# Block 0's VectorE and GpSimd work in another order, a reordered head, and the logits bias as a TensorE product

## What is computed

```python
h = gelu(embedding @ W0 + b0); h = gelu(h @ W1 + b1)
att = softmax(h @ W2 + b2)                       # 64 sequences x 8 kernels
agg_w = einsum('bk,koi->boi', att, weight[..., 0]); agg_b = att @ bias_k
hid = einsum('boi,bih->boh', agg_w, x) + agg_b[:, :, None]     # x: (64, 32, 512)

s = relu(hid @ up_w) ** 2                        # 512 -> 1024
shared = s @ down_w                              # 1024 -> 512
lat = hid @ fc1_w                                # 512 -> 256
routed = (lat @ expert_w) * sum(top2(hid @ gate_w)) @ fc2_w
out = x + layernorm(shared + routed) * ln_gamma + ln_beta
```

## Time and profile before

| what | value |
|---|---|
| median of 3 runs | 257.34 us (257.14 to 257.56) |
| the profiled execution: its time, its span | 257.82 us, 256.0 us |
| TensorE matmul busy | 248.1 us (97%), 1293 instructions |
| VectorE, ScalarE, GpSimd busy | 159.0 us (62%), 81.4 us (32%), 47.5 us (19%) |
| chain that ended last, by engine | TensorE 83%, VectorE 9%, issue 3%, DMA 2%, ScalarE 1% |

### The profile page before, as it was taken

The page is one execution under the profiler, slowest core; times in us unless marked ns, Lnnn a source line. Parts: engine busy times, 40 slices in busy tenths (PEclk is TensorE's granted clock), DMA queues, the critical chain, the costliest instruction groups (busy, mean ns, idle before and its releaser), DMA issues.

```text
span 256.0 us, 3526 instructions
## 1 busy us (share of the span) xinstructions
PE 248.1 (97%) x1293; PEld 207.0 (81%) x1293; DVE 159.0 (62%) x270; ACT 81.4 (32%) x141; POOL 47.5 (19%) x48
## 2 busy tenths in 40 slices
PE   7899999999999999999999999999999999999992
PEld 6778877988888888888888888888888888788891
DVE  4699999964448974544446984474444963406453
ACT  5567747530113344321111443331111355202100
POOL 2404083001115320001113501001111700001110
PEclk9999999999999999999999999999999999999998
DMA  6992805001111400001100220000111100000211
GB/s 146 352 358 93 320 0 165 3 0 44 41 41 41 141 25 0 3 0 42 41 38 16 80 112 0 0 0 0 41 41 44 42 0 0 3 0 2 80 44 41
DMA packets 10428, 15.60 MB, mean 61 GB/s; under 512 B 1072, under 2 KB 4912, under 8 KB 10416
## 3 DMA queue, kind: packets, MB, share of 16 engines
q1 hardware_dynamic: 9968, 15.33, 17.7%
q10 hardware_dynamic: 448, 0.11, 0.2%
HBM read 11.23 MB, written 4.20 MB: 60 GB/s over the span
## 4 chain that ended last, share of the span: by engine, by line
PE 83%; DVE 9%; issue 3%; DMA 2%; ACT 1%; POOL 0%; SPq 0%; POOLq 0%; DVEq 0%; ACTq 0%
PE ps L913 25%; PE ps L915 25%; PE ps L914 25%; PE ps L888 4%; DVE sq_lo L694 3%; DMA experts_sb<-in_experts_dram 2%; PE ps L980 2%; PE ps L841 2%; DVE y_buf L656 1%; DVE up_lo L626 1%; DVE down_lo L771 1%; PE ps L894 1%; DVE agg L663 0%; ACT up_hi L471 0%; DVE sq_hi L692 0%
## 5 line engine op out<-in xcount | busy, mean ns | idle before, releaser
L913 PE MATMUL ps<-down_hi,sq_hi 128*128 128x512 f32 (+1 forms) x136 | 51.2, 377 | 0.0
L914 PE MATMUL ps<-down_lo,sq_hi 128*128 128x512 f32 (+1 forms) x136 | 51.2, 377 | 0.0
L915 PE MATMUL ps<-down_hi,sq_lo 128*128 128x512 f32 (+1 forms) x136 | 51.2, 376 | 0.0
L913 PE MATMUL ps<-h_hi,up_hi 128*128 128x512 f32 x126 | 49.1, 390 | 0.2 <-DVE h_lo L647 0.2
L914 PE MATMUL ps<-h_lo,up_hi 128*128 128x512 f32 x126 | 49.0, 389 | 0.0
L915 PE MATMUL ps<-h_hi,up_lo 128*128 128x512 f32 x126 | 49.0, 389 | 0.0
L423 POOL TENSOR_TENSOR rstd<-mv,half 128x1 f32<-128x1 f32 x16 | 15.3, 954 | 158.1 <-DVE mv L726 153.1
L522 ACT ACTIVATE relu_sq<-ps 128x512 f32<-128x512 f32 x32 | 19.1, 597 | 58.2 <-PE ps L915 44.3
L719 DVE TENSOR_TENSOR y_buf<-ps,y_buf 128x512 f32<-128x512 f32 x15 | 10.4, 692 | 39.5 <-PE ps L915 39.3
L692 DVE CAST sq_hi<-relu_sq 128x512 fp32r<-128x512 f32 x32 | 22.6, 705 | 15.8 <-ACT relu_sq L524 15.2
L694 DVE TENSOR_TENSOR sq_lo<-relu_sq,sq_hi 128x512 fp32r<-128x512 f32 x32 | 30.9, 965 | 1.1
(11 more groups left out here) (136 smaller groups left out, 300.4 us busy)
## 6 DMA issues: line engine op xcount, KB each, us to landing
out_dram<-late SPq DMA_DIRECT2D x15, 256.0 KB, 2.0
x_cur<-in_x_dram SPq DMA_DIRECT2D x3, 1024.0 KB, 5.2
late<-in_down_w_dram SPq DMA_DIRECT2D x4, 512.0 KB, 5.0
late<-in_up_w_dram SPq DMA_DIRECT2D x3, 512.0 KB, 8.2
x_cur<-in_x_dram SPq DMA_DIRECT2D x2, 512.0 KB, 6.3
agg_b<-aggb_dram SPq DMA_DIRECT2D x1, 768.0 KB, 5.9
latents_sb<-in_latents_dram SPq DMA_DIRECT2D x1, 528.0 KB, 5.3
experts_sb<-in_experts_dram SPq DMA_DIRECT2D x1, 512.0 KB, 5.2
```

The source lines that it names most:

```text
L913: nc.tensor.matmul(dst, a_hi, b_hi, start=first, stop=False)
L914: nc.tensor.matmul(dst, a_hi, b_lo, start=False, stop=False)
L915: return nc.tensor.matmul(dst, a_lo, b_hi, start=False, stop=last)
```

## The change

It consists of these parts.

- The load of `b2_rows` and VectorE's addition go. `bias_sb`, the load of bias_k, has behind each row of bias_k eight more columns, of which row 0 holds b2 and the others are zero. A product of ones (`idle`) with these eight rows starts the accumulation of `LOGIT`, and the product with w2 ends it. The maximum and the exponential read `LOGIT` itself.
- Three idle products are added behind `WEIGHT_T`, and the third `fold_expert` call moves behind the transpose.
- `FIRST_BIAS` moves ahead of the last chunk of the first mix's first half. Behind it, on ScalarE and VectorE, the second piece of the up weights moves behind the copy of the bias and behind the first h.
- The up products of m = 0 and 1 of block 0 do the two products with `h_hi` before the one with `h_lo`, in all four chunks (before: in the first alone), and wait for `up_lo` piece by piece.
- In block 0, VectorE does `fc1_lo` and the first `x_plus_beta` itself, and squares, aggregate and down weights come in another order; on ScalarE the `down_high` calls come behind m = 3, 4 and 5, and `q_high` behind m = 6 and 7. Blocks 1 to 3 are as before.

```diff
-            sp.dma_start(b2_rows[:, :], kernels[0, C * C + C:C * C + C + K].partition_broadcast(NB)
-                         ).then_inc(b2_loaded, 16)
...
@@ GpSimd @@
-            pool.wait_ge(fc1_hi_ready, 1)
-            nc.gpsimd.tensor_tensor(fc1_lo[:, :, :], fc1_raw, fc1_hi[:, :, :].bitcast(fp32),
-                                    ALU.subtract).then_inc(fc1_lo_ready, 1)
...
-            def pool_block(b):
+            next_mix(0)
+            pool.wait_ge(mix_ready, G)
+            inverse_deviations(0)
+            with pool.Fori(1, NBLK - 1) as b:
                 x_plus_beta(b)
                 next_mix(b)
...
@@ ScalarE @@
-            act.wait_ge(logit_ready, 1)
             act.wait_ge(max_done, 1)
-            nc.scalar.activation(att_exp[:, :], logit_sb[:, :], ACT.Exp, bias=neg_max[:, :],
+            nc.scalar.activation(att_exp[:, :], LOGIT, ACT.Exp, bias=neg_max[:, :],
                                  accum_out=exp_sum[:, :]).then_inc(exp_done, 1)
...
             split_up(0)
-            split_up(1)
             act.wait_ge(bias_spread, 1)
             nc.scalar.copy(agg_b[:, 0:TOK], FIRST_BIAS).then_inc(bias_copied, 1)
+            split_up(1)
...
             for m in range(IC):
                 relu_square(0, m)
-                if m < 4:
-                    down_high(m)
+                if m == 3:
+                    down_high(0)
+                    down_high(1)
                 if m in (4, 5):
-                    q_high(m - 4)
+                    down_high(m - 2)
+                if m in (6, 7):
+                    q_high(m - 6)
...
@@ VectorE @@
-            dve.wait_ge(b2_loaded, 16)
-            nc.vector.tensor_tensor(logit_sb[:, :], LOGIT, b2_rows[:, :], ALU.add).then_inc(logit_ready, 1)
-            dve.wait_ge(logit_ready, 1)
-            nc.vector.tensor_reduce(neg_max[:, :], logit_sb[:, :], AX.X, ALU.max, negate=True).then_inc(max_done, 1)
+            nc.vector.tensor_reduce(neg_max[:, :], LOGIT, AX.X, ALU.max, negate=True).then_inc(max_done, 1)
...
             split_up(0)
-            split_up(1)
             dve.wait_ge(bias_copied, 1)
             first_mix_bias(0)
+            split_up(1)
             first_mix_bias(1)
...
+            def first_x_plus_beta():
+
+                dve.wait_ge(affine_loaded, 16)
+                dve.wait_ge(first_x_loaded, 16)
+                dve.wait_ge(x_loaded, 16)
+                dve.wait_ge(down_hi_ready, 2)
+                dve.wait_ge(down_lo_ready, 2)
+                nc.vector.tensor_tensor(x_beta, x_cur[:, :, :], beta_b.unsqueeze(1).to_broadcast([P, TB, HID]),
+                                        ALU.add).then_inc(xbeta_ready, 1)
...
@@ TensorE @@
+            pe.wait_ge(bias_loaded, 16)
+            nc.tensor.matmul(LOGIT, idle[0:K, 0:NB].bitcast(fp32), b2_row, start=True, stop=False)
             pe.wait_ge(gelu_done, 2)
-            nc.tensor.matmul(LOGIT, hid2[:, :], w2_sb, start=True, stop=True).then_inc(logit_done, 1)
+            nc.tensor.matmul(LOGIT, hid2[:, :], w2_sb, start=False, stop=True).then_inc(logit_done, 1)
...
+            stay_warm(3)
             pe.wait_ge(experts_loaded[0], 16)
             fold_expert(0, 0, 0)
             fold_expert(0, 0, 1)
-            fold_expert(1, 0, 0)
...
-            for c in range(HC):
+            for c in range(HC - 1):
                 first_mix_tiles(c, (0, 1))
             pe.wait_ge(attb_lo_ready, 2)
             pe.wait_ge(attP_copied, 1)
             nc.tensor.matmul(FIRST_BIAS, ones[:, :], bias_rows, start=True, stop=True).then_inc(bias_spread, 1)
+            first_mix_tiles(HC - 1, (0, 1))
...
-                pe.wait_ge(up_lo_ready, 2)
-                pe.wait_ge(h_hi_ready, 1)
...
+                for c in range(HC):
+                    pe.wait_ge(h_hi_ready, c + 1)
+                    for m in (0, 1):
+                        cols = slice(m * P, (m + 1) * P)
+                        pe.wait_ge(up_lo_ready, m + 1)
+                        nc.tensor.matmul(ps[:, UP_BANK[m], :], up_hi[:, c, cols], h_hi[:, c, :],
+                                         start=(c == 0), stop=False)
+                        nc.tensor.matmul(ps[:, UP_BANK[m], :], up_lo[:, c, cols], h_hi[:, c, :],
+                                         start=False, stop=False)
                     pe.wait_ge(h_lo_ready, c + 1)
                     for m in (0, 1):
-                        last = up_chunk(m, c)
+                        last = nc.tensor.matmul(ps[:, UP_BANK[m], :], up_hi[:, c, m * P:(m + 1) * P], h_lo[:, c, :],
+                                                start=False, stop=(c == HC - 1))
```

More of the change, by code:

```diff
@@ L148, in adaln_ffn_kernel @@
         bias_raw = bias_sb[:, 0:C]
+        b2_row = bias_sb[0:K, C:C + K]
         idle = sb("idle", [P, P], f32r)
-        b2_rows = sb("b2_rows", [NB, K])
-        logit_sb = sb("logit_sb", [NB, K])
         sel_g = sb("sel_g", [NB, G])
@@ L212, in adaln_ffn_kernel @@
         experts_loaded = [sem(f"experts_loaded{i}") for i in range(2)]
-        b2_loaded = sem("b2_loaded")
         x_loaded = sem("x_loaded")
@@ L240, in adaln_ffn_kernel @@
         padded = sem("padded")
-        logit_ready = sem("logit_ready")
         weightT_done = sem("weightT_done")
@@ L414, in x_plus_beta @@
                 pool.wait_ge(x_loaded, 16 * (b + 1))
-                wait_past(pool, final_done, TB * b)
+                pool.wait_ge(final_done, TB * b)
                 nc.gpsimd.tensor_tensor(x_beta, x_cur[:, :, :],
@@ L425, in _ @@
             pool.wait_ge(affine_loaded, 16)
-            pool.wait_ge(first_x_loaded, 16)
-            pool.wait_ge(down_hi_ready, 2)
-            pool.wait_ge(down_lo_ready, 2)
-            def pool_block(b):
+            next_mix(0)
+            pool.wait_ge(mix_ready, G)
+            inverse_deviations(0)
+            with pool.Fori(1, NBLK - 1) as b:
                 x_plus_beta(b)
@@ L433, in pool_block @@
                 inverse_deviations(b)
-            pool_block(0)
-            with pool.Fori(1, NBLK - 1) as b:
-                pool_block(b)
             x_plus_beta(NBLK - 1)
@@ L772, in down_low, with fc1_low @@
                                         ALU.subtract).then_inc(down_lo_ready, 1)
+            def fc1_low():
+                dve.wait_ge(fc1_hi_ready, 1)
+                nc.vector.tensor_tensor(fc1_lo[:, :, :], fc1_raw, fc1_hi[:, :, :].bitcast(fp32),
+                                        ALU.subtract).then_inc(fc1_lo_ready, 1)
+            def first_x_plus_beta():
[6 more added lines that the diff above has]
+                                        ALU.add).then_inc(xbeta_ready, 1)
+            split_square(0, 0)
             spread_aggregate(0)
+            split_square(0, 1)
             sum_aggregate(0)
-            for m in range(IC):
-                split_square(0, m)
-                if m < 4:
-                    down_low(m)
-                if m in (4, 5):
-                    q_low(m - 4)
+            split_square(0, 2)
+            fc1_low()
+            split_square(0, 3)
+            down_low(0)
+            down_low(1)
+            first_x_plus_beta()
+            split_square(0, 4)
+            down_low(2)
+            split_square(0, 5)
+            down_low(3)
+            split_square(0, 6)
+            q_low(0)
+            split_square(0, 7)
+            q_low(1)
             latent_low(0)
@@ L875, in _ @@
                                 ident[0:NB, 0:NB]).then_inc(attT_done, 1)
+            fold_expert(1, 0, 0)
             fold_expert(1, 0, 1)
@@ L881, in _ @@
             fold_expert(1, 1, 1).then_inc(q_done, 1)
-            pe.wait_ge(bias_loaded, 16)
             pe.wait_ge(attT_copied, 1)
@@ L925, in up_first_block @@
                 pe.wait_ge(bias_copied, 1)
-                pe.wait_ge(up_lo_ready, 2)
-                pe.wait_ge(h_hi_ready, 1)
-                for m in (0, 1):
-                    cols = slice(m * P, (m + 1) * P)
-                    nc.tensor.matmul(ps[:, UP_BANK[m], :], up_hi[:, 0, cols], h_hi[:, 0, :], start=True, stop=False)
-                    nc.tensor.matmul(ps[:, UP_BANK[m], :], up_lo[:, 0, cols], h_hi[:, 0, :], start=False, stop=False)
-                pe.wait_ge(h_lo_ready, 1)
-                for m in (0, 1):
-                    nc.tensor.matmul(ps[:, UP_BANK[m], :], up_hi[:, 0, m * P:(m + 1) * P], h_lo[:, 0, :],
-                                     start=False, stop=False)
-                for c in range(1, HC):
+                for c in range(HC):
[7 more added lines that the diff above has]
+                                         start=False, stop=False)
                     pe.wait_ge(h_lo_ready, c + 1)
                     for m in (0, 1):
-                        last = up_chunk(m, c)
+                        last = nc.tensor.matmul(ps[:, UP_BANK[m], :], up_hi[:, c, m * P:(m + 1) * P], h_lo[:, c, :],
+                                                start=False, stop=(c == HC - 1))
                         if c == HC - 1:
```

## The result

The changed kernel takes 260.16 us, median of 22 runs (257.77 to 261.44), against 257.55 us (257.14 to 259.49) for the kernel before on the same chip: a ratio of 1.0088 (95% interval 1.0070 to 1.0107). It is slower by 2.6 us, where 1.1 us of gain was forecast. Of the 22 executions of the changed kernel two took 257.8 and 258.2 us, nine 259.3 to 259.9 (the profiled one among them) and eleven 260.4 to 261.4.

The account below looks back on a forecast made before the run. TensorE's work bounds the kernel from block 0's down product on, so only head and block 0 can gain: 0.53 + 0.6 = 1.13 us, from 257.34 to 256.2 us; range for 8 in 10, 255.8 to 256.9.

Parts of the forecast that it names:

- The b2_rows load goes: ... All later SP issues move 0.61 us up: Head: without the 2 KB load the experts are issued at 1.19, not 1.80, and land at 6.4; folds start at 6.7.
- bias_k "covered by 0.7": Head, logits: bias_k, waited for earlier, lands at 4.5 while TensorE is busy until 5.2, so 0.7 us to spare.
- The slower rival: Logits: bias row late behind its 2.5 KB load; landing at 6.4 eats the whole gain, at 7.5 gives 258.4; 5%.
- The experts land no earlier: Head: expert landing set by the engines, not the issue; folds start at 7.06, gain 0.8 in all, 256.55 us; 17%.
- Head, 0.53: Head to block 0's up products: up chunk 2 starts at about 21.45 instead of 21.99, a gain of 0.53 us.
- Block 0, 0.6: Block 0: moving GpSimd's fc1_lo and first x plus beta to VectorE removes TensorE's 0.6 us gap before the latent product.
- the waits did not only change their names: Rival: TensorE's gaps come back at the gate or the next mix, 257.3 us; 8%.
- that rival (8%): Block 0: VectorE is held by GpSimd's copies (257.1 us) or by an addition of 4.67 us (256.8); 8%.
- By that rule ... the 1.31 us down_lo does not: Block 0: the skill's VectorE-GpSimd exclusion disagrees with down_lo's 1.31 us beside copies; forecast adds 0.3 us, rule would give 257.1.
- The addition of 64x8 on VectorE goes; I count nothing: Logits: removing VectorE's bias addition gains nothing, because the exponential behind it waits for its table load.

Follow-up runs that it names:

- mlp first: Changed kernel with the second half of the mlp load issued first on ScalarE's queue, ahead of the 32 KB of kernels: 257.84 us, ratio 1.0032.
- SP held: Changed kernel, no 2 KB load, with SP waiting for VectorE's memset of the ones before issuing the expert load: 257.14 us, ratio 0.9972.
- mlp on SP: Changed kernel with the second half of the mlp load issued on SP's queue ahead of the experts, not on ScalarE's: 256.96 us, ratio 1.0001.
- nine idle products: Changed kernel with nine idle products ahead of the second layer instead of three, loads unchanged: 258.30 us, ratio 1.0021.
- logits bias alone: Kernel before with only the 2 KB load and the addition replaced by a TensorE product for the logits bias: 260.42 us, ratio 1.0096.
- kernel before with idle products: Kernel before with only the three idle products added behind the transposed kernels: 257.56 us, ratio 0.9989.
- both reorderings: Changed kernel's new orders of head and block 0, with b2 load and addition as before and no added idle products: 256.96 us, ratio 0.9968.

## Why the prediction was wrong

**The step that failed** is "The b2_rows load goes: ... All later SP issues move 0.61 us up", as far as it was costed as a gain alone. The earlier issue was seen, and the experts landed even before their forecast (5.7, not 6.4). What the head waits for was taken from the profile of before with every other landing unchanged, and `mlp_sb`'s was not even written down, since nothing waited for it there: it landed at 3.4, 0.5 us before the GELU. An expert load issued together with it delayed it by 2.2 us.

What the runs show in place of this step is an order. A load issued ahead of the 512 KB keeps its time, one issued with it or behind it does not:

| kernel | experts issued | load, issued | landed after |
|---|---|---|---|
| before | 1.80 | mlp_sb 1.19 | 2.2 |
| after | 1.19 | mlp_sb 1.19 | 4.4 |
| mlp first | 1.19 | mlp_sb 0.74 | 2.5 |
| mlp first | 1.19 | h_full 1.18 | 4.8 |
| SP held | 1.60 | mlp_sb 1.19 | 2.1 |
| SP held | 1.60 | bias_sb 1.69 | 4.5 |
| before | 1.80 | bias_sb 1.70 | 2.8 |
| mlp on SP | 1.66 | bias_sb 1.19 | 2.3 |

The pause of 0.41 us and the moved issue undo it with no load added, so the 2 KB load was never a cost: it was what kept the expert load behind the 69 KB.

**Where 3.2 us come from.** The kernel with mlp on SP (256.96, first mix at 11.46 in the chain), the one with nine idle products (258.30, at 12.82) and the changed kernel (260.16 and 260.73, at 14.06 and 15.39) form a ladder. The wait for the load costs 1.34 us (258.30 less 256.96). The rest, 1.9 to 2.4 in the medians, is TensorE's lower clock level: six more idle products fill only half of the same wait, and this part is gone from all twelve executions (258.85 at most).

It comes in two amounts. In the execution of 259.48 TensorE had reached its upper level and lost it from 8 to 11, and the first mix is 1.24 behind that with nine idle products. In that of 260.87 it had not reached it before 12, and the mix is 2.57 behind. These are one profile each of the two larger groups of times. The mean granted clocks of all 22 executions fit them: 0.991 or 0.992 in eight of the nine at 259.3 to 259.9, and 0.998 to 1.000, like that of 260.87, in all eleven from 260.4.

Two things stay open. Kernels without a late load climb late too in some executions (four of eleven with mlp on SP, 2.0 us above the others), so not all of the larger amount need come from the wait. And not every wait costs clock: one of 1.12 us did not (logits bias alone), one of 1.15 did (SP held).

**The other steps.**
- *bias_k "covered by 0.7"*: wrong. It landed at 6.4 and not 4.5. In the changed kernel the late GELU hid it; in two others TensorE waited 1.0 and 1.15 us for it. The slower rival (5%) had the landing right (6.4) and the mechanism, a small load late beside an earlier expert load, but the load that cost was another. Its argument against itself, "2.8 now", was a duration of a queue state that the change removed.
- *The experts land no earlier* (17%): refuted, 5.7.
- *Head, 0.53*: mis-sized. Where the loads are in time, up chunk 2 comes 0.41 to 0.48 earlier than in the earlier trace rows (21.58 and 21.51), with the first mix late because ATT_P waits for `att_tiles` (7.76 with mlp on SP) and takes 0.49 and not 0.22. In the medians it is worth nothing: 256.96 with it, 256.89 without. The profile of before had the experts landing after 5.2 us. In the kernel before with idle products they landed after 4.2, and the old order of the head reached chunk 2 at 21.42, ahead of both reordered ones:

```profile
experts_sb<-in_experts_dram SPq DMA_DIRECT2D x1, 512.0 KB, 4.2
...
21.42 0.39 PE L914 MATMUL ps<-h_hi,up_hi 128*128 128x512 f32 x1
```

  By these profiles the new order gains where the experts land late and nothing where they land early. The forecast took one late landing as the rule.
- *Block 0, 0.6*: right, 0.59 in the profile and 0.8 in the median, so the waits did not only change their names (8%). VectorE's 2.28 was 2.29; `down_lo` beside the copies took 1.31, so they do not hold VectorE for long, and that rival (8%) fell.
- *"By that rule ... the 1.31 us down_lo does not"*: misread. The prediction took 0.75 us (2.98 for four) as a copy's own length. In the kernel before one takes 0.28 at 93.98 us, where VectorE is idle, and 0.57 where it starts inside an `sq_lo`:

```profile
94.61 0.69 DVE L694 TENSOR_TENSOR sq_lo<-relu_sq,sq_hi 128x512 fp32r<-128x512 f32 x1
...
94.89 0.57 POOL L411 COPY mix<-agg 32x128 f32 x1 [0.16 <-POOL mix L411]
```

  So the copies look like the ones that are held, and a `down_lo` that loses at most the rest of a copy of 0.3 us fits the rule as well. The forecast by the row was right all the same.
- *"The addition of 64x8 on VectorE goes; I count nothing"*: not contradicted, and no run isolates it. In the changed kernel too the exponential (8.27) starts right behind its table load (6.86 to 8.14) and the warm-up (8.16).

## What to carry to other kernels

When a change moves a large DMA, write down every load in flight beside it with its issue, landing and slack, those that nothing waits for in particular, and price each as if it doubled. Issue the small loads that the first instructions need ahead of the first large one, on whichever queue. A wait of TensorE in the first microseconds costs itself and can cost the clock: fill it with idle products before judging what it is worth. A gain of the size by which one load's landing moves nearly the same head (0.57 us of chunk 2 here) wants medians of the part alone, and more than one profile. The fastest here is the kernel before with block 0's new order alone, at 256.89, which the runs don't tell from the one with mlp on SP and the one with both reorderings (256.96 each).

## What was unexpected of the hardware

- A 69 KB load on ScalarE's queue took 4.4 us instead of 2.2 beside a 512 KB load of SP's queue issued at the same time. In the list of DMA queues for 2 to 3 us (packets, MB, share of 16 engines; q10 carries ScalarE's loads) the changed kernel has moved 278 of the 448 packets of that queue

```profile
q10 hardware_dynamic: 278, 0.04, 23.4%
```

  and the kernel before 429 of its 448:

```profile
q10 hardware_dynamic: 429, 0.10, 53.3%
```

  The Trainium skill (DMA: Bandwidth & Descriptors, "Queues, rings and completion order") has each DMA engine take the queues in turn, packet by packet. The trace agrees in kind: from 3 to 4 us the changed kernel moves (q1 carries SP's loads)

```profile
q1 hardware_dynamic: 100, 0.20, 72.1%
q10 hardware_dynamic: 77, 0.04, 23.2%
```

  so about one packet for one, but 2 KB against 0.5. The load is 144 packets (q10 has 448 with it, 304 with mlp on SP). If each lets one of 2 KB pass, 0.36 MB go by, 1.0 to 1.7 us at the 355 to 211 GB/s of these stretches, where 69 KB alone take 0.2 to 0.3: an estimate of 0.8 to 1.4 us of delay. The runs show 2.2; what holds the last packets was not found.
- The granted clock in the record stood at 1.00 in executions whose idle products and folds took 1.6 to 1.9 times as long as at the upper level (0.99 against 0.60, 1.91 against 1.03), up to 10 or 12 us. The Trainium skill (TensorE: Matmul & The Clock Gate, "Seeing it yourself") warns that recorded clock events may be unreliable; this trace agrees, and the durations of equal products are the better witness.
